# Borders of expert runs: half tiles, two side by side in the array, their weights copied ahead

## The chip, the core and the metric

The kernel runs on one core of a Trainium2 chip. Its engines are TensorE (PE in the profile, with its weight loads as PEld), VectorE (DVE), ScalarE (ACT), GpSimd (POOL) and SyncE (SP). The metric is the device time of one execution in microseconds; lower is better.

## The reference

A gated cross-attention block over `x` of shape (4, 512, 256) is followed by a feed-forward layer, which itself holds self-attention, an RMS norm, a shared gated network and a routed network. Only the routed network and the end matter here. Each of the 2048 tokens has two of eight experts, both of one group of four:

```python
p_expert = e_probs * g_prob
topv, topi = jax.lax.top_k(p_expert, TOPK)
w = jnp.zeros((S, E), flat.dtype).at[jnp.arange(S)[:, None], topi].set(topv)
h = _swiglu(flat @ W1_shared)
routed = jnp.zeros_like(shared)
for e in range(E):
    routed = routed + h @ W2_experts[e] * w[:, e:e + 1]
out = x + (shared + routed).reshape(Bb, Tt, C)
return _rmsnorm(out, norm2_w)
```

`h` has 512 columns and each `W2_experts[e]` is 512x256.

## The kernel before

The pair of experts of a token is its class: 2 groups with 6 pairs each, 12 classes. The kernel sorts the tokens by class (a count by matrix products, an indirect DMA that scatters the rows, a load of the sorted rows) and cuts the sorted rows into 16 tiles of 128 tokens (`NT`). Classes are ordered so that in each of two lanes (first and second expert) the expert stays the same over a run of classes. There are 14 runs and so 12 borders between runs of a lane (`BORDERS`, pairs of a class and a lane).

For each tile two *base* products are made, one for each lane, with the experts that hold at the tile's first row (`ebase`, read into registers by PE). A token of that tile that belongs to a later run gets weight 0 in the base product (`wb` against `wrest`). What is missing is added by the borders. A border lies in some tile that is known only at run time (`btile`); this tile's `h` is copied by ACT to a fixed place (`hb`, four places, 11 copies in all since two borders share a class), PE multiplies all of its 128 rows with the expert behind the border (an expert known in advance), and DVE adds the product to the sorted rows with the weights `wsel`, which are 0 for all rows but those of the run.

Sizes: `h` is stored as `hS`, 128 partitions x 16 tiles x 4 x 128 columns in fp32. A product is four matrix products over 4 x 128 rows of the contraction, each of 256 columns, and an fp32 matrix product shows as two instructions. So a base tile is 16 instructions and a pair of borders 16.

Each engine has its own list of instructions, written out by hand and coupled by semaphores. The order of PE's work at the end stands in the list `LAST`: the routed networks of four batches (`routed`), then base tile 0, the six pairs of borders, base tiles 1 to 15. `ETILES` numbers the products in that order over the eight banks of PSUM, and PE takes a bank when the product eight places earlier has been emptied, by the engine named in `ETILES` ("A" is ACT, "V" is DVE). DVE does, in order: base 0, the borders, the sum of squares of tile 0, then for each further tile `base(t)`, `finish(t - 1)`, `squares(t)`. `base` adds the two lanes (lines 1406 and 1413), `squares` sums the squares (1418) and multiplies by the norm's weights (1427), `finish` applies the row scale and the residual (1433). GpSimd computes the row scale (787) and stores the finished rows by an indirect DMA (793).

ACT at this stage makes the tanh of each routed product (line 967), and at the very end the border copies (999 loads the tile's number into a register, 1000 copies). Behind the last gate (`gate`, lines 1381 and 1384 on DVE) there is no other work on ACT. `runs` on DVE (1349 to 1358) computes the tables from the class counts; it is done before the first routed product.

Of the kernel before, what the change touches and what calls it, by code (L numbers as in the profile page):

```python
# [14 lines left out]
P = 128  # L15
# [20 lines left out]
def flamingo_block(nc, x, ctx_in, g_xattn, g_ffn, wq, bq, wk, bk, wv, bv,  # L36
# [138 lines left out]
    COPIES = list(dict.fromkeys(c_ for c_, _ in BORDERS))  # L175
# [54 lines left out]
    with es:  # L230
# [30 lines left out]
        tabs = sb("tabs", [P, 6, NCLS], F32)  # L261
# [53 lines left out]
        hb = [t_.rearrange("p (c j) -> p c j", c=HT) for t_ in th]  # L315
# [20 lines left out]
        btile = sb("btile", [P, NCLS], I32)  # L336
        leq = sb("leq", [P, NT, NCLS], F32)
# [3 lines left out]
        wrest = sb("wrest", [P, NT, 2], F32)  # L341
        wsel = sb("wsel", [P, 2, 8], F32)
        tok = sb("tok", [P, NT], U32)
        ssq = sb("ssq", [P, NT], F32)
        rs = sb("rs", [P, NT], F32)

# [69 lines left out]
        s_hb = sem("border_tile_copied")  # L416
# [42 lines left out]
        BORDER_USED = {c_: EAT["borders", j_ // 2] + 1 for j_, (c_, _) in enumerate(BORDERS)}  # L459

        WRAW = [src[2][:, 0:CT, :], src[3][:, 0:CT, :], sa[0][:, 0:CT, :]]

        N_CST = 14 + 3 * (len(STARTS[0]) + len(STARTS[1]))
# [6 lines left out]
        def _(sp):  # L471
# [154 lines left out]

            for a in range(8):
                sp.wait_ge(s_st[a], 16 * NT // 8)
# [3 lines left out]
        def _(pool):  # L632
# [68 lines left out]
            def constants():  # L701
# [14 lines left out]
                pool.iota(tstart[:], pattern=[[P, NT]], base=0, channel_multiplier=0,  # L716
# [88 lines left out]
        def _(act):  # L805
# [169 lines left out]

            for name, *at in LAST:
                if name in ("turn", "sorted"):
                    end_turn(name, *at)
                elif name in ("nets", "routed"):
                    for p in range(HT):  # L980
                        if at[1] <= 2 * p < at[2]:
                            tanh((B * (name == "routed") + at[0]) * HT + p, name, at[0], p)
                    if (name, at[0]) == ("nets", 1) and at[2] == NETT:
# [20 lines left out]
        def _(dve):  # L1004
# [341 lines left out]
            def runs():  # L1346
# [4 lines left out]
                link(V.tensor_scalar(bs[:], bs[:], float(NT * P - 1), None, ALU.min))  # L1351
# [3 lines left out]
                link(V.tensor_copy(btile[:], bs[:]))  # L1355
                mark(V.tensor_reduce(rbe[:], t, AX.X, ALU.add))
                link(V.tensor_scalar(btile[:], btile[:], 7, None, ALU.logical_shift_right))
                mark(V.tensor_copy(ebase[:], rbe[:, 2:4, :]))
                ready(s_run)

            def sorted_weights():
# [4 lines left out]
                link(V.tensor_tensor(wb[:], rn, rbe[:, 0:2, :].rearrange("p x t -> p t x"), ALU.is_equal))  # L1366
                link(V.tensor_tensor(wb[:], wb[:], wv, ALU.mult))
                link(V.tensor_tensor(wrest[:], wv, wb[:], ALU.subtract))
                for lane in range(2):
                    t = tmp[:, 0:8 * NT].rearrange("p (r t) -> p r t", r=8)  # L1370
                    link(V.tensor_tensor(t, rn[:, :, lane].unsqueeze(1).to_broadcast([P, 8, NT]),
# [16 lines left out]
            def border(j):  # L1388
                r = end_full("borders", j)
                for i in range(2):  # L1390
                    c, lane = BORDERS[2 * j + i]
                    at = dve.value_load(btile[0:1, c:c + 1], min_val=0, max_val=NT - 1)
                    y = srows[:, bass.ds(at, 1), 0:D].rearrange("p o c -> p (o c)")
                    x = RUN[lane][c] - 1
                    ins = V.scalar_tensor_tensor(out=y, in0=r[:, i * D:(i + 1) * D], scalar=wsel[:, lane, x:x + 1], in1=y,
                                                 op0=ALU.mult, op1=ALU.add)
                    if i:
                        ins.then_inc(s_ev, 1)
                        end_settle("borders", j)
                    else:  # L1400
                        link(ins)
# [90 lines left out]
        def _(pe):  # L1492
# [352 lines left out]
            def borders():  # L1845
                for j in range(len(BORDERS) // 2):
                    o = end_take("borders", j)
                    for i in range(2):
                        c, lane = BORDERS[2 * j + i]
                        at = COPIES.index(c)  # L1850
                        pe.wait_ge(s_hb, at + 1)
                        last = product(o[:, i * D:(i + 1) * D], [(hb[at % 4][:, k, :], w2[:, k, CLASSES[c][lane], :]) for k in range(HT)])
                    last.then_inc(s_ef, 1)
# [83 lines left out]
```

## Time and profile before

| | |
|---|---|
| median of 3 runs | 771.36 us (771.14 to 774.34) |
| the profiled execution | 771.94 us |
| its span, first to last instruction | 769.8 us |
| busy in the span | PE 738.4, DVE 514.1, ACT 408.4, POOL 217.7 us |
| borders on PE | 20.88 us |
| the 15 base tiles behind them on PE | 51.96 us |

Times in the rows are microseconds from the span's start unless marked ns; `x16` is a number of instructions. In a timeline row the last bracket is the idle time of that engine before the instruction and what ended it. PE's ends are modelled.

### The profile page before, as it was taken

To read this page: it belongs to the slowest core of one execution; us is meant where nothing else is said; L and a number is where in the kernel's file an instruction comes from. 1 tells how busy PE (TensorE), PEld (TensorE's weight loads), DVE (VectorE), ACT (ScalarE), POOL (GpSimd) and SP (SyncE) were. 2 spreads that over 40 slices of the span, in tenths; PEclk is the share of its full clock that TensorE was granted. 3 is DMA by queue.
4 is the path that set the end of the run, shared out by engine and by line. 5 is a ranking of instruction groups with operands and counts; after the bars stand their busy time and mean duration, and the time that the engine had idled before them with its cause. 6 is when DMAs were issued, how large, how long until landed. Compare 5 with 4: busy or idle time off the path is not lost.

```text
span 769.8 us, 10338 instructions
## 1 busy us (share of the span) xinstructions
PE 738.4 (96%) x3512; PEld 336.5 (44%) x3512; DVE 514.1 (67%) x774; ACT 408.4 (53%) x768; POOL 217.7 (28%) x327
## 2 busy tenths in 40 slices
PE   8889999999999999999999999999999999999995
PEld 5432343343233233233423432424544756468884
DVE  5698748847968878878797789771466122533765
ACT  4456867867758766875775867676211122222000
POOL 5252133223315405303321510010104631400444
PEclk9999999999999999999999999999999999999998
DMA  9519243325224414512331243005002565000011
GB/s 263 182 46 297 70 124 112 83 66 194 57 49 163 120 42 124 152 43 82 124 84 42 96 111 84 1 2 190 29 1 107 191 201 164 1 1 0 33 38 41
DMA packets 51891, 73.31 MB, mean 95 GB/s; under 512 B 7808, under 2 KB 42880, under 8 KB 51840
## 3 DMA queue, kind: packets, MB, share of 16 engines
q1 hardware_dynamic: 47248, 63.80, 28.4%
q0 software_dynamic: 2816, 8.46, 2.9%
q10 hardware_dynamic: 1776, 0.40, 0.3%
q8 instruction: 29, 0.48, 0.3%
q14 instruction: 22, 0.18, 0.1%
HBM read 45.04 MB, written 27.33 MB: 94 GB/s over the span
## 4 chain that ended last, share of the span: by engine, by line
PE 75%; DVE 13%; ACT 5%; issue 3%; DMA 3%; SPq 0%; POOL 0%; POOLq 0%; DVEq 0%; ACTq 0%
PE ps L1534 35%; PE ps L1693 12%; PE ps L1729 11%; PE ps L1665 10%; DVE negm L1180 8%; ACT hS L931 3%; PE ps L1529 2%; DVE bst L1058 1%; PE ps L1593 1%; PE ps L1679 1%; DMA rows<-in_L_xattn_wq_dram 1%; DMA w<-mTs 1%; PE ps L1588 1%; PE ps L1624 0%; DMA scrq<-mix 0%
## 5 line engine op out<-in xcount | busy, mean ns | idle before, releaser
L1180 DVE TENSOR_REDUCE negm<-ps 128x2 f32<-128x1024 f32 x256 | 303.6, 1220 | 72.7 <-PE ps L1665 64.9
L931 ACT ACTIVATE hS<-ps 128x512 f32<-128x512 f32 x512 | 280.7, 605 | 114.5 <-PE ps L1729 112.5
L1729 PE MATMUL ps<-w 98*128 98x512 bf16 x512 | 169.3, 383 | 6.4 <-DVE qk L1113 1.9
L1665 PE MATMUL ps<-w 96*128 96x512 bf16 x512 | 152.7, 379 | 8.0 <-DVE negm L1180 4.9
L1693 PE MATMUL ps<-hS,mix 128*17 128x512 f32 x1024 | 134.7, 598 | 0.2
L1729 PEld LDWEIGHTS ps<-w 98*128 98x128 bf16 x512 | 43.6, 96 | 157.3 <-ACT hS L931 94.8
L1665 PEld LDWEIGHTS ps<-w 96*128 96x128 bf16 x512 | 47.2, 98 | 60.1 <-DVE negm L1180 12.8
L1381 DVE SCALAR_TENSOR_TENSOR ctxs<-qk,ps 128x512 f32<-128x512 f32 x32 | 22.0, 687 | 71.5 <-ACT qk L967 46.0
L967 ACT ACTIVATE qk<-ps 128x512 f32<-128x512 f32 x32 | 19.1, 597 | 76.2 <-PE ps L1534 73.3
L1534 PE MATMUL ps<-w,hS 128*128 x256 | 55.6, 379 | 0.0
L1534 PEld LDWEIGHTS ps<-w,hS 128*128 128x128 f32 x256 | 48.6, 190 | 7.0 <-issue 0.5
L654 POOL TENSOR_TENSOR mdif<-bst 128x4 f32<-128x4 f32 x12 | 2.5, 205 | 150.6 <-DVEq L1020 150.6
L677 POOL TENSOR_TENSOR qk<-qk,mix 128x1024 f32<-128x1024 f32 x14 | 29.8, 2129 | 47.8 <-ACT mix L851 47.4
L692 POOL TENSOR_SCALAR hS<-hS,tg 128x256 f32<-128x256 f32 x16 | 14.9, 928 | 92.8 <-DVEq L1206 92.8
L1693 PEld LDWEIGHTS ps<-hS,mix 128*17 128x17 f32 x1024 | 17.0, 95 | 53.9 <-ACT hS L931 29.9
L672 POOL TENSOR_TENSOR qk<-qk,hT 128x1024 f32<-128x1024 f32 x8 | 18.8, 2348 | 76.1 <-DVEq L1020 76.1
L682 POOL TENSOR_TENSOR mix<-qk,mix 128x1024 bf16<-128x1024 f32 x14 | 29.9, 2134 | 21.9 <-ACT mix L855 20.8
L1534 PE MATMUL ps<-fout,hS 128*128 128x256 f32 x128 | 28.7, 380 | 1.5 <-issue 1.5
L1384 DVE SCALAR_TENSOR_TENSOR hS<-ctxs,ps 128x512 f32<-128x512 f32 x32 | 22.0, 687 | 11.8 <-PE ps L1534 10.6
L1534 PE MATMUL ps<-cT,fin 128*128 128x512 f32 x64 | 28.4, 594 | 0.3 <-ACT cT L960 0.3
L1534 PE MATMUL ps<-rope_sb,fin 128*128 128x512 f32 x64 | 28.4, 594 | 0.0
L1534 PE MATMUL ps<-wT,fin 128*128 128x512 f32 x64 | 28.1, 592 | 0.0
(217 smaller groups left out, 852.7 us busy)
## 6 DMA issues: line engine op xcount, KB each, us to landing
w<-scrq SPq DMA_DIRECT2D x32, 384.0 KB, 4.2
scrk<-mix SPq DMA_DIRECT2D x24, 256.0 KB, 2.3
scrq<-mix SPq DMA_DIRECT2D x16, 384.0 KB, 3.3
w<-scrk SPq DMA_DIRECT2D x32, 192.0 KB, 2.9
scrq<-mix SPq DMA_DIRECT2D x24, 256.0 KB, 2.6
w<-scrk SPq DMA_DIRECT2D x32, 128.0 KB, 3.0
w<-in_L_ffn_W_experts_dram SPq DMA_DIRECT2D x8, 512.0 KB, 8.2
mix<-scrf SPq DMA_DIRECT2D x4, 528.0 KB, 4.2
```

The costliest lines, as they stand in the source:

```text
L672: link(pool.tensor_tensor(qk[X][:], qk[X][:], rb[X], ALU.add))
L677: link(pool.tensor_tensor(qk[X][:], qk[X][:], parts[X][:, 0], ALU.subtract))
L682: link(pool.tensor_tensor(parts[X][:, 2], qk[X][:], parts[X][:, 1], ALU.subtract))
L931: nc.scalar.activation(prob[:, kt % PROB_SLOTS, s % HG, :], slot_bank(("unit", u)), ACT.Exp, scale=SC).then_inc(s_exp, 1)
L967: nc.scalar.activation(th[k % 4], end_full(f"{name}{b}", 2 * p), ACT.Tanh, scale=0.5).then_inc(s_th, 1)
L1180: V.tensor_reduce(negm[:, gi % 2, h, 2 * t2:2 * t2 + 2], ps[:, bank:bank + 2, :], AX.X, ALU.max, negate=True).then_inc(s_re, 1)
L1381: V.scalar_tensor_tensor(out=uu[:, k % 2, :], in0=th[k % 4], scalar=1.0, in1=end_full(f"{name}{b}", 2 * p), op0=ALU.add, op1=ALU.mult).the ...
L1384: V.scalar_tensor_tensor(out=hS[:, b * TT:(b + 1) * TT, p, :], in0=uu[:, k % 2, :].rearrange("p (t j) -> p t j", t=TT), scalar=0.5, in1=en ...
L1534: last = MM(o, w, r, start=(j == 0), stop=(j == len(terms) - 1))
L1665: last = MM(ps[:, bank + t, :], qs[0:STK, g, h, tt * P:(tt + 1) * P], ks[0:STK, g, h, :], start=True, stop=True)
L1693: last = MM(ps[32 * h:32 * h + VM, 6, :], vp[n % 2][:, kt, g * HG + h, :], prob[:, kk % PROB_SLOTS, h, :], start=(kt == 0), stop=(kt == TT ...
L1729: MM(o, ks[:, g, h, kt * P:(kt + 1) * P], qs[:, g, h, :], start=True, stop=True).then_inc(s_sT, 1)
```

## The change

Base tiles take the experts at their middle row (`tstart` begins at 64) instead of the first. A run that ends in a tile then misses rows either ahead of the border in the tile's first half, or behind it in the second half; only one half of 64 rows (`bhalf`) needs a correction. Which expert this half needs, the one ahead of the border or behind it, now depends on the half (`bexpi`). So each border takes a half tile of `h` (64 columns of the array) and two borders stand side by side in the array's columns 0 to 63 and 64 to 127, products of the two in turn.

Since the expert is known only at run time, ACT copies its weights (128 x 1024 elements) to a fixed place for each border (`wplace`), nine of them between the tanhs of the routed products, three after the half-tile copies at the end. The half-tile copies are 12 to 12 places, each with two register loads. ACT empties PSUM for the borders, two copies of 64 rows a pair, and SP doubles the 64 rows into the other 64 partitions by two DMAs a pair; DVE adds from there (`corr`). Base tile 1 moves ahead of the borders on PE and DVE.

```diff
-    LAST += [("base", 0), ("borders",)] + [("base", t_) for t_ in range(1, NT)]
+    LAST += [("base", 0), ("base", 1), ("borders",)] + [("base", t_) for t_ in range(2, NT)]
...
-            take_end("borders", range(len(BORDERS) // 2), "V")
+            take_end("borders", range(len(BORDERS) // 2), "A")
...
+            for q in range(len(BORDERS) // 2):
+                sp.wait_ge(s_ea, end_emptied("borders", q)[1])
+                sp.dma_start(corr[2 * q][HP:P, :], corr[2 * q][0:HP, :]).then_inc(s_br[q], 16)
+                sp.dma_start(corr[2 * q + 1][0:HP, :], corr[2 * q + 1][HP:P, :]).then_inc(s_br[q], 16)
...
-                pool.iota(tstart[:], pattern=[[P, NT]], base=0, channel_multiplier=0,
+                pool.iota(tstart[:], pattern=[[P, NT]], base=HP, channel_multiplier=0,
...
+                        pool.memset(tabs[:, 6 + lane, c:end], float(CLASSES[c][lane])).then_inc(s_cst, 1)
...
+            def border_weights(i):
+                if i == 0:
+                    act.wait_ge(s_run, 1)
+                    act.wait_ge(s_w2, 16 * NE)
+                if i < 2:
+                    act.wait_ge(s_ef, EAT[f"nets{B - 1}", NETT - 1] + 1)
+                elif i < 5:
+                    act.wait_ge(s_ef, EAT[f"routed{i - 2}", NETT - 1] + 1)
+                elif i < 9:
+                    act.wait_ge(s_y, B)
+                else:
+                    act.wait_ge(s_ef, EAT[f"routed{B - 1}", NETT - 1] + 1)
+                c, lane = BORDERS[i]
+                e = act.value_load(bexpi[0:1, lane, c:c + 1], min_val=0, max_val=NE - 1)
+                nc.scalar.activation(wplace[i], w2[:, :, bass.ds(e, 1), :].rearrange("p k o n -> p k (o n)"), ACT.Copy).then_inc(s_wc, 1)
+            WEIGHTS_AT = {(0, 1): [0], (0, 3): [1], (1, 1): [2], (2, 1): [3], (3, 0): [4], (3, 1): [5, 6], (3, 2): [7, 8]}
...
-            act.wait_ge(s_run, 1)
             act.wait_ge(s_ev, gate_done(2 * B * HT - 1))
-            for j, c in enumerate(COPIES):
-                if j >= 4:
-                    act.wait_ge(s_ef, BORDER_USED[COPIES[j - 4]])
+            for i, (c, lane) in enumerate(BORDERS):
                 at = act.value_load(btile[0:1, c:c + 1], min_val=0, max_val=NT - 1)
-                nc.scalar.activation(hb[j % 4], hS[:, bass.ds(at, 1)].rearrange("p o c j -> p (o c) j"), ACT.Copy).then_inc(s_hb, 1)
+                h = act.value_load(bhalf[0:1, c:c + 1], min_val=0, max_val=1)
+                nc.scalar.activation(hb[i], halves[:, bass.ds(at, 1), :, bass.ds(h, 1), :].rearrange("p t c h j -> p (t c) (h j)"),
+                                     ACT.Copy).then_inc(s_hb, 1)
+            for i in range(9, len(BORDERS)):
+                border_weights(i)
+            for q in range(len(BORDERS) // 2):
+                r = end_full("borders", q)
+                nc.scalar.activation(corr[2 * q][0:HP, :], r[0:HP, 0:D], ACT.Copy).then_inc(s_bc, 1)
+                nc.scalar.activation(corr[2 * q + 1][HP:P, :], r[HP:P, 0:D], ACT.Copy).then_inc(s_bc, 1)
+                act.wait_ge(s_bc, 2 * (q + 1))
+                act.sem_inc(s_ea, 1)
...
+            def border(i):
+                c, lane = BORDERS[i]
+                if i % 2 == 0:
+                    dve.wait_ge(s_br[i // 2], 32)
+                at = dve.value_load(btile[0:1, c:c + 1], min_val=0, max_val=NT - 1)
+                y = srows[:, bass.ds(at, 1), 0:D].rearrange("p o c -> p (o c)")
+                x = RUN[lane][c] - 1
+                link(V.scalar_tensor_tensor(out=y, in0=corr[i], scalar=wsel[:, lane, x:x + 1], in1=y, op0=ALU.mult, op1=ALU.add))
...
             base(0)
-            for j in range(len(BORDERS) // 2):
-                border(j)
+            base(1)
+            for i in range(len(BORDERS)):
+                border(i)
             squares(0)
-            for t in range(1, NT):
+            squares(1)
+            finish(0)
+            for t in range(2, NT):
...
+                for q in range(len(BORDERS) // 2):
+                    o = end_take("borders", q)
+                    pe.wait_ge(s_hb, 2 * q + 2)
+                    pe.wait_ge(s_wc, 2 * q + 2)
+                    for k in range(HT):
+                        for j in range(2):
+                            i = 2 * q + j
+                            last = MM(o[j * HP:(j + 1) * HP, 0:D], hb[i][:, k, :], wplace[i][:, k, :], start=(k == 0), stop=(k == HT - 1))
```

Left out of the diff: the places of `wplace`, `hb` and `corr` in tiles that are free by then, `runs` with some ten more operations of 12 or 24 elements for `bhalf` and `bexpi`, and `sorted_weights` with two more of 32 elements (rows ahead of the border now belong to the correction too).

## Rows read from the trace of the kernel before

**Rows 1.** The page's first part: busy time, share of the span, instructions.
```profile
PE 738.4 (96%) x3512; PEld 336.5 (44%) x3512; DVE 514.1 (67%) x774; ACT 408.4 (53%) x768; POOL 217.7 (28%) x327
```

**Rows 2.** The chain that ended last, from 560 us: start, us, what.
```profile
667.82 89.70 PE ps L1534 x376
```

**Rows 3.** Busy time by window: us, then each engine, clock, DMA share, GB/s.
```profile
691.74:712.40 20.66, 20.66 (x97) 18.21 (x96) 6.24 (x14) 4.41 (x7) 0.07 (x1) 1.00 0.00 0
```

**Rows 4.** Timeline, PE from base tile 0 on: start, us, instruction.
```profile
684.83 3.62 PE L1534 MATMUL ps<-w,hS 128*128 x16
...
688.28 20.88 PE L1534 MATMUL ps<-w,qk 128*128 128x256 f32 x96
...
709.00 51.96 PE L1534 MATMUL ps<-w,hS 128*128 x240
```

**Rows 5.** Timeline, DVE from the first squares to base tile 14.
```profile
711.77 0.43 DVE L1418 CUSTOM_DVE_ANT_0 tmp<-mix 128x256 f32<-128x256 f32 x1
...
712.54 0.42 DVE L1427 TENSOR_TENSOR hT<-mix,n_bc 128x256 f32<-128x256 f32 x1 [0.34 <-DVE ssq L1418]
712.88 0.48 DVE L1406 SCALAR_TENSOR_TENSOR mix<-ps,wb,mix 128x256 f32<-128x256 f32 x1
...
713.92 0.49 DVE L1433 SCALAR_TENSOR_TENSOR hT<-hT,rs,rows 128x256 f32<-128x256 f32 x1
...
715.17 0.46 DVE L1427 TENSOR_TENSOR hT<-mix,n_bc 128x256 f32<-128x256 f32 x1
...
757.55 0.48 DVE L1406 SCALAR_TENSOR_TENSOR mix<-ps,wb,mix 128x256 f32<-128x256 f32 x1 [0.70 <-PE ps L1534]
```

**Rows 6.** Timeline, PE in the router: the same round and the next.
```profile
555.52 0.59 PE L1789 MATMUL ps<-cT,fg 128*32 128x512 f32 x1
...
555.54 0.59 PE L1789 MATMUL ps<-nT,fg 128*32 128x512 f32 x1
555.95 0.59 PE L1789 MATMUL ps<-cT,fg 128*32 128x512 f32 x1
```

**Rows 7.** Timeline, the last gate and ACT's border copies.
```profile
685.10 0.69 DVE L1384 SCALAR_TENSOR_TENSOR hS<-ctxs,ps 128x512 f32<-128x512 f32 x1 [0.41 <-PE ps L1534]
686.75 2.57 ACT L1000 ACTIVATE qk<-hS 128x512 f32 x4 [2.79 <-DVE hS L1384]
...
700.40 0.63 ACT L1000 ACTIVATE qk<-hS 128x512 f32 x1 [0.31 <-issue]
```

**Rows 8.** Line 999, ACT's sequencer: ns min/median/max, first and last start.
```profile
L999 ACTq TENSOR_LOAD <-btile x11: 272/277/489, 685.9 to 703.0; - x11
L999 ACTq FUSED_REGOPS  x11: 152/152/185, 686.4 to 703.3; - x11
```

**Rows 9.** Line 855, ACT's copies of 128x1024.
```profile
L855 ACT ACTIVATE mix<-qk x14: 1047/1058/1088, 36.5 to 437.8; 128x1024 bf16<-128x1024 f32 x14
```

**Rows 10.** Timeline, ACT: one of the 16 routed tanhs.
```profile
679.93 0.60 ACT L967 ACTIVATE qk<-ps 128x512 f32<-128x512 f32 x1 [2.84 <-PE ps L1534]
```

**Rows 11.** Line 527, SP's DMAs of 256 KB: the issue, and the landing.
```profile
L527 SPq DMA_DIRECT2D scrk<-mix x24: 359/360/1435, 16.1 to 443.8; - x24
...
DMA to landing us min/median/max: 2.1/2.3/7.8
```

**Rows 12.** DMA issues: KB each, median us to landing.
```profile
w<-scrk SPq DMA_DIRECT2D x32, 64.0 KB, 3.3
```

**Rows 13.** Line 1392, DVE's sequencer in the borders.
```profile
L1392 DVEq TENSOR_LOAD <-btile x12: 298/302/554, 692.0 to 710.5; - x12
```

**Rows 14.** Timeline, DVE: the first pair of borders.
```profile
693.02 0.48 DVE L1395 SCALAR_TENSOR_TENSOR mix<-ps,wsel,mix 128x256 f32 x1 [3.42 <-issue]
694.27 0.48 DVE L1395 SCALAR_TENSOR_TENSOR mix<-ps,wsel,mix 128x256 f32 x1 [0.77 <-DVE mix L1395]
```

**Rows 15.** Timeline, DVE: the first routed gate after the runs.
```profile
623.54 0.69 DVE L1381 SCALAR_TENSOR_TENSOR ctxs<-qk,ps 128x512 f32<-128x512 f32 x1 [23.04 <-PE ps L1534]
```

**Rows 16.** Timeline, POOL: the first work after the constants.
```profile
67.56 0.94 POOL L692 TENSOR_SCALAR hS<-hS,tg 128x256 f32<-128x256 f32 x1 [9.98 <-DVEq L1206]
```

More of the change, by code:

```diff
@@ L173, in flamingo_block @@
     assert sorted(BORDERS) == sorted((c_, lane) for lane in range(2) for c_ in STARTS[lane][1:])
-    COPIES = list(dict.fromkeys(c_ for c_, _ in BORDERS))
+    HP = P // 2
     ETILES = []
@@ L260, in flamingo_block @@
         upto = sb("upto", [NT * NCLS // 2, 2, NT * NCLS + NCLS], F32)
-        tabs = sb("tabs", [P, 6, NCLS], F32)
+        tabs = sb("tabs", [P, 8, NCLS], F32)
         tstart = sb("tstart", [P, NT], F32)
@@ L314, in flamingo_block @@
         ostage = hT[:].rearrange("p k (u c) -> p (k u) c", u=2)
-        hb = [t_.rearrange("p (c j) -> p c j", c=HT) for t_ in th]
+        halves = hS[:].rearrange("p t c (h j) -> p t c h j", h=2)
+        hb = [t_[:, i * HT * HP:(i + 1) * HT * HP].rearrange("p (c j) -> p c j", c=HT)
+              for t_ in th + [uu[:, 0, :], uu[:, 1, :]] for i in range(2)]
+        fins = [fin[:, i].rearrange("p k n -> p (k n)")[:, j * HT * D:(j + 1) * HT * D].rearrange("p (k n) -> p k n", k=HT)
+                for i in range(2) for j in range(2)]
+        wplace = fins[0:2] + [t_.rearrange("p k n -> p (k n)").rearrange("p (k n) -> p k n", k=HT) for t_ in xT[0:3]]
+        wplace += [rows[:, 4 * i:4 * i + 4, 0:D] for i in range(4)] + fins[2:4]
+        wplace += [xT[3].rearrange("p k n -> p (k n)").rearrange("p (k n) -> p k n", k=HT)]
         lg = sb("lg", [P, NT, NR], F32)
@@ L336, in flamingo_block @@
         btile = sb("btile", [P, NCLS], I32)
+        bhalf = sb("bhalf", [P, NCLS], I32)
+        bpos = sb("bpos", [P, 3, NCLS], F32)
+        bexp = sb("bexp", [P, 2, NCLS], F32)
+        bexpi = sb("bexpi", [P, 2, NCLS], I32)
         leq = sb("leq", [P, NT, NCLS], F32)
@@ L341, in flamingo_block @@
         wrest = sb("wrest", [P, NT, 2], F32)
+        bno = sb("bno", [P, NT, 2], F32)
         wsel = sb("wsel", [P, 2, 8], F32)
@@ L345, in flamingo_block @@
         rs = sb("rs", [P, NT], F32)
+        corr = [ostage[:, i, :] for i in range(8)] + [tmp[:, i * D:(i + 1) * D] for i in range(3)] + [oT[:, 0:D]]
         ps = es.enter_context(nc.psum_tensor("ps", [P, 8, L], F32))
@@ L415, in flamingo_block @@
         s_ssh = sem("sorted_shared_loaded")
-        s_hb = sem("border_tile_copied")
+        s_hb = sem("border_half_copied")
+        s_wc = sem("border_weights_copied")
+        s_bc = sem("border_product_copied")
+        s_br = [sem(f"border_rows_doubled{q}") for q in range(len(BORDERS) // 2)]
         s_ss = sem("squares_summed")
@@ L456, in gate_half @@
             return end_emptied(f"{name}{b}", 2 * p)[1]
-        BORDER_USED = {c_: EAT["borders", j_ // 2] + 1 for j_, (c_, _) in enumerate(BORDERS)}
         WRAW = [src[2][:, 0:CT, :], src[3][:, 0:CT, :], sa[0][:, 0:CT, :]]
-        N_CST = 14 + 3 * (len(STARTS[0]) + len(STARTS[1]))
+        N_CST = 14 + 4 * (len(STARTS[0]) + len(STARTS[1]))
         def group_inst(gi):
@@ L982, in _ @@
                             tanh((B * (name == "routed") + at[0]) * HT + p, name, at[0], p)
+                            for i in WEIGHTS_AT.get((at[0], p), []) if name == "routed" else []:
+                                border_weights(i)
                     if (name, at[0]) == ("nets", 1) and at[2] == NETT:
@@ L1350, in runs @@
                                      bs[:].unsqueeze(1).to_broadcast([P, NT, NCLS]), ALU.is_ge))
-                link(V.tensor_scalar(bs[:], bs[:], float(NT * P - 1), None, ALU.min))
+                link(V.tensor_scalar(bs[:], bs[:], -1.0, 0.0, ALU.add, ALU.max))
                 t = tmp[:].rearrange("p (x t c) -> p x t c", x=4, t=NT)
@@ L1354, in runs @@
                                      tabs[:, 0:4, :].unsqueeze(2).to_broadcast([P, 4, NT, NCLS]), ALU.mult))
-                link(V.tensor_copy(btile[:], bs[:]))
+                mark(V.tensor_copy(btile[:], bs[:]))
+                link(V.tensor_copy(bhalf[:], bs[:]))
                 mark(V.tensor_reduce(rbe[:], t, AX.X, ALU.add))
-                link(V.tensor_scalar(btile[:], btile[:], 7, None, ALU.logical_shift_right))
+                mark(V.tensor_scalar(btile[:], btile[:], 7, None, ALU.logical_shift_right))
+                link(V.tensor_scalar(bhalf[:], bhalf[:], 6, None, ALU.logical_shift_right))
                 mark(V.tensor_copy(ebase[:], rbe[:, 2:4, :]))
+                mark(V.tensor_copy(bpos[:, 0], btile[:]))
+                link(V.tensor_copy(bpos[:, 1], bhalf[:]))
+                link(V.scalar_tensor_tensor(out=bpos[:, 2], in0=bpos[:, 0], scalar=-2.0, in1=bpos[:, 1], op0=ALU.mult, op1=ALU.add))
+                link(V.tensor_scalar(bpos[:, 2], bpos[:, 2], 1.0, None, ALU.subtract))
+                link(V.tensor_tensor(bexp[:], tabs[:, 2:4, :], bpos[:, 2:3, :].to_broadcast([P, 2, NCLS]), ALU.mult))
+                link(V.tensor_tensor(bexp[:], bexp[:], tabs[:, 6:8, :], ALU.add))
+                mark(V.tensor_copy(bexpi[:], bexp[:]))
+                link(V.tensor_scalar(bpos[:, 2], bpos[:, 2], 1.0, None, ALU.add))
+                mark(V.tensor_copy(bhalf[:], bpos[:, 2]))
                 ready(s_run)
@@ L1365, in sorted_weights @@
                 mark(V.tensor_copy(tok[:], srows[:, :, D + 4]))
-                link(V.tensor_tensor(wb[:], rn, rbe[:, 0:2, :].rearrange("p x t -> p t x"), ALU.is_equal))
+                rb_ = rbe[:, 0:2, :].rearrange("p x t -> p t x")
+                mark(V.tensor_tensor(bno[:], rn, rb_, ALU.is_lt))
+                link(V.tensor_tensor(wb[:], rn, rb_, ALU.is_equal))
+                mark(V.tensor_tensor(bno[:], bno[:], rn, ALU.add))
                 link(V.tensor_tensor(wb[:], wb[:], wv, ALU.mult))
@@ L1386, in gate @@
                                        op0=ALU.mult, op1=ALU.mult).then_inc(s_ev, 1)
[L1388 to L1401, printed above, removed]
+            def border(i):
[6 more added lines that the diff above has]
+                link(V.scalar_tensor_tensor(out=y, in0=corr[i], scalar=wsel[:, lane, x:x + 1], in1=y, op0=ALU.mult, op1=ALU.add))
             def base(t):
@@ L1845, in borders @@
             def borders():
[L1846 to L1852, printed above, removed]
+                for q in range(len(BORDERS) // 2):
[6 more added lines that the diff above has]
+                            last = MM(o[j * HP:(j + 1) * HP, 0:D], hb[i][:, k, :], wplace[i][:, k, :], start=(k == 0), stop=(k == HT - 1))
                     last.then_inc(s_ef, 1)
```

3 lines of the change are left out of this document (2 added, 1 removed).

## The prediction

> **What bounds the kernel now.** I read the page's engine line first, then the chain of waits over the last 210 us, then the timeline of each engine from 684 us on. TensorE (PE) is busy in nearly the whole span [rows 1], and the chain of the last stage is one piece of PE products from 667.82 to 757.52 us [rows 2]. In that piece lie the last products of the routed nets, base tile 0, the six pairs of borders and base tiles 1 to 14 and half of 15. The stretch of the borders is full of PE, while VectorE (DVE) works 6 us and ScalarE (ACT) 4 us of its 21 [rows 3]. PE spends 20.88 us on the 96 border products, 3.45 us a pair, and 51.96 us on the 15 later base tiles, 3.46 us each [rows 4].
>
> So a saving on PE counts only as far as DVE can follow, and DVE's own pace decides that. DVE sits idle 0.70 us before each late base tile, until PE's product is there; tile 14 begins at 757.55. A base tile that DVE had not to wait for is tile 1: it begins at 712.88, 0.34 us after the start of the operation before it (L1427), and its own L1427 begins at 715.17 [rows 5]. So DVE alone needs 715.17 - 712.88 + 0.34 = 2.63, say 2.65 us a tile: it can win back 0.8 us a tile on PE, and no more.
>
> **PE's part.** Each pair becomes two products of 64 columns in the two halves of the array. No row shows 64 columns. The nearest is the router, four products of 32 columns each: their instructions begin at 555.52 to 555.54, and the next round at 555.95 [rows 6], so four run in the time of one, 0.43 us for 512 elements. For two halves of 256 elements I take one in the time of two: 20.88 becomes 10.4 us. The bounds are 10.4 and 20.9 (no gain). Base tile 1 now comes ahead of the borders, which start two tiles after 684.83, at 691.74 [rows 4], and without waits would end at 702.1.
>
> **ACT's part, which I think sets the end.** Before, ACT made 11 copies of whole tiles, four of them before PE needed the first. Now it makes, after the last gate: 12 copies of half tiles, each with two indices loaded from memory into registers; three copies of weights (borders 9, 10, 11); and only then the 12 copies of products out of PSUM. These all stand in order on one engine. Step by step:
>
> The last gate ends at 685.10 + 0.69 = 685.79 and ACT's first copy starts at 686.75; four copies take 2.57 us [rows 7]. As the copy itself is 0.63, the step from one to the next is (2.57 - 0.63) / 3 = 0.65. 
> Of weights, ACT has 128x1024 copies at 1.06 us [rows 9]. One load (0.65), then three copies: 700.6 + 0.65 + 3.18 = 704.4. The nine other weight copies go between the tanhs, where ACT idles 2.84 us after each 0.60 us [rows 10]; one or two copies (1.1 or 2.1 us, their index loads under the tanh before) fit. Without that cover each would cost 1.06.
>
> The product copies are 64x256 out of PSUM: from 0.60 for 512 elements [rows 10], less 256 elements at (1.06 - 0.63) / 512 us, 0.39 each. Two of them and ACT's signal are ready at 705.2.
>
> **The DMA's part.** SyncE doubles each pair's rows with two transfers of 64 KB. Its shortest transfers land 2.1 us after issue, median 2.3, and an issue takes 0.36 [rows 11]; transfers of this size took 3.3 in a queue of others [rows 12]. Nothing else is on the queue here, so I take 2.2 + 0.4 = 2.6: rows doubled at 707.8. Bounds 2.5 and 3.7. Queued behind that wait on SP are only later pairs and the last waits for the stores. Later pairs are ready every 0.8 us, faster than DVE takes them.
>
> **DVE's part.** DVE has been idle since base tile 1 (some 14 us). Its first border needs an index load, about 1.0 us after the wait; borders then follow at 694.27 - 693.02 = 1.25 us, because each load waits for the chain behind the border before [rows 13, 14]. The reads now come from SBUF instead of PSUM; DVE's L1433, which reads two SBUF tiles, also takes 0.49 [rows 5], so the price stays. Twelve borders: 707.8 + 1.0 + 11 x 1.25 + 0.48 = 723.0. Then squares of tiles 0 and 1 (1.11 us each, as 711.77 to 712.88 [rows 5]) and finish 0 (0.49, with its waits 0.65) bring base tile 2 to 725.9. Twelve tiles at 2.65 make 31.8: base tile 14 at 757.7, against 757.55 now. Everything behind it is as it was.
>
> To this I add two holes of 0.31 us, as the one that ACT shows under "issue" among eleven copies [rows 7], since ACT's list of instructions here grows two to three times: 0.6. Sum: +0.15 + 0.6, some 0.8 us. PE meanwhile waits for weights 9 to 11, ends the borders at 704.4 + 1.7 = 706.1 and base tile 14 at 751.2, so about 6 us of its gain lie idle before DVE's tile 14. PSUM does not hold PE: base tile 10 needs tile 2's bank, which DVE empties near 727, and PE is there at 733.7.
>
> **Costed at nothing.** The longer computation of the runs on DVE, some ten operations of 0.2 us, falls before an idle time of 23.04 us [rows 15]. The 14 new memsets on GpSimd, 0.1 us each, fall before an idle time of 9.98 us [rows 16]. Two more operations on the sorted rows' weights (0.4) fall into DVE's waits for PE.
>
> **A rule against the change.** ACT's index loads take 277 ns and DVE's 302 ns [rows 8, 13]. The Trainium skill, page "DMA: Bandwidth & Descriptors", section "Latency and other measured facts", gives a floor of about 600 ns for a tensor_load; by that the path's 25 loads on ACT and 12 on DVE would add 25 x 0.32 + 12 x 0.30 = 11.7 us, an estimate of 784.5 us. Both rows are about half of that floor, so the trace does not bear it out; the third rival below is its mechanism, priced from rows.
>
> **Rivals.**
>
> *PE stays the bound.* Then the full 10.4 us count: 761.5. DVE would have to reach base tile 2 by 757.5 - 10.4 - 31.8 = 715.3 us, 10.6 us before my sum. The order on ACT alone speaks against it: its first product copy comes no sooner than the three late weights. Chance 0.03.
>
> *The second index load is hidden.* At 0.65 a copy, ACT is ready 12 x 0.56 = 6.7 us sooner and DVE stays the bound: 772.7 - 6.7 = 766.0. For it: ACT's load begins while the copy before it runs. Against it: the step of 0.65 is already as long as its register work. Chance 0.05.
>
> *Slower: the index loads at their first price.* The first load of each engine took 489 (ACT) and 554 ns (DVE) [rows 8, 13]. If loads of three alternating tables always cost that, 25 x 0.21 + 12 x 0.25 = 8.3 us more: 781. It passes the 0.5% once the 37 loads are longer by 0.08 us each. Against it: the medians, 277 and 302, over eleven and twelve loads at changing addresses. Chance 0.10.
>
> *The halves don't run side by side.* Then PE ends the borders at 712.4 and base tile 14 at 757.5, level with DVE's chain: no change or 1 us more, about 772. The time does not show it; the timeline of PE would. Chance 0.05.
>
> *My sum:* 0.77.
>
> **The numbers.** The sum goes onto the profiled execution: 771.94 us, of which 769.8 are span. With 0.8 more it is 772.7. The runs' median, 771.36, lies 0.6 below that execution, so the forecast is 772.2. Within 0.5% (about what a measurement of this kernel can tell from no change) means 767.5 to 775.2. Faster than that: the first two rivals, 0.07 (the second lies just beyond the bound, so not all of its 0.05 counts). Slower: 0.13, the third rival's 0.10 and 0.03 for the sum with several upper ends together (transfers at 3.7, +1.1; a third and fourth hole, +0.6; loads 0.05 longer, +1.8). Same: 0.80. The range that leaves out no more than 2 in 10 is 768.0 to 776.3: below, half of the second load hidden (-3.4) and a little; above, those upper ends.
>
> **What would show it.** PE: border instructions in twos, a pair in 1.7 us, a wait of some 3.5 us before the fifth pair and 0.4 to 2 before the sixth. ACT: copies of half tiles 1.2 us apart from 687.3 to 700.6, then three copies of weights, the first product copy at 704.4. DVE: idle until about 708.8, borders 1.25 apart to 723, then base tiles 2.65 apart with no wait for PE. I am wrong if DVE still waits for PE in the base tiles, if the half-tile copies come closer than 1.0 or farther than 1.4 us apart, or if the first border on DVE begins before 705 or after 712.

## The result, and the profile after

| | before | after |
|---|---|---|
| median, 20 runs each | 772.62 us | 775.04 us (772.47 to 778.54) |
| ratio to before | | 1.0034, 95% interval 1.0023 to 1.0046 |
| span of the profiled execution | 769.8 us | 772.8 us |

The changed kernel is 2.6 us slower by the ratio (0.0034 x 772.6). The forecast was 0.8 us slower, "same" within 0.5%, range 768.0 to 776.3.

I split the 3.0 us between the two spans at points that both traces have. Behind the end of the last gate the change behaves nearly as predicted. More than half of the difference between these two executions lies ahead of that gate, where no step of the prediction looks. Outside its span the changed kernel needs 0.4 us less (774.58 - 772.8 = 1.78 us, where the kernel before has 771.94 - 769.8 = 2.14), so the two profiled times lie 2.6 us apart; the profile does not show why.

| point | before | after | after, a second execution |
|---|---|---|---|
| last gate ends | 685.79 | 687.43 | 685.71 |
| from there to base tile 14 on DVE | 71.76 | 72.89 | 72.62 |
| from there to the end of the span | 12.25 | 12.48 | 12.57 |
| span | 769.8 | 772.8 | 770.9 |

The first part of the page of the changed kernel answers to [rows 1]: PE is 6.2 us less busy, DVE has 13 instructions more, ACT 25 and POOL 14.

```profile
PE 732.2 (95%) x3512; PEld 327.3 (42%) x3512; DVE 514.3 (67%) x787; ACT 423.1 (55%) x793; POOL 218.6 (28%) x341
```

**PE.** This is the timeline of PE in the changed kernel: base tiles 0 and 1, then the first pairs of borders and the fifth.

```profile
686.47 7.07 PE L1599 MATMUL ps<-w,hS 128*128 x32
693.47 1.95 PE L1918 MATMUL ps<-fin,qk 128*64 128x256 f32 x16
695.25 0.38 PE L1918 MATMUL ps<-cT,qk 128*64 128x256 f32 x1
695.25 0.38 PE L1918 MATMUL ps<-rope_sb,qk 128*64 128x256 f32 x1
695.46 0.38 PE L1918 MATMUL ps<-cT,qk 128*64 128x256 f32 x1
...
696.97 0.38 PE L1918 MATMUL ps<-wT,qk 128*64 128x256 f32 x1
...
704.54 0.40 PE L1918 MATMUL ps<-rows,ctxs 128*64 128x256 f32 x1 [3.95 <-ACT fin L1013]
...
705.67 0.63 PE L1918 MATMUL ps<-rows,ctxs 128*64 128x256 f32 x1
```

The second pair begins at 695.25 and the third at 696.97: 1.72 us a pair where [rows 4] have 3.45. The two products of a pair start together (695.25 and 695.25), and the next instruction of the first product follows 0.21 later, as in a product that has the array to itself. Then PE waits 3.95 us for the first of the three late copies of weights on ACT (L1013). Behind that wait an instruction shows 0.63 instead of 0.38 us from 705.67 on. The windows (columns as in [rows 3]) say why: the granted clock is 1.00 ahead of the wait, and behind it 0.68 on average over a stretch that ends with full-speed instructions again, so in part of it PE ran at the lower of its two levels (1.2 instead of 2.4 GHz). Here that costs nothing, since DVE is late anyway. The sixth pair follows the fifth without a wait.

```profile
693.50:700.50 7.00, 7.00 (x65) 4.47 (x64) 0.97 (x2) 2.45 (x6) 0.00 (x0) 1.00 0.00 0
704.50:709.80 5.30, 5.25 (x32) 3.65 (x32) 0.00 (x0) 4.72 (x11) 0.00 (x0) 0.68 0.15 36
```

**ACT.** The timeline of ACT in the changed kernel, half-tile copies (L1042), late weights (L1013) and the first product copy (L1048); it answers to [rows 7].

```profile
688.71 0.42 ACT L1042 ACTIVATE qk<-hS 128x256 f32 x1 [3.10 <-issue]
689.97 0.42 ACT L1042 ACTIVATE qk<-hS 128x256 f32 x1 [0.85 <-issue]
...
702.68 0.42 ACT L1042 ACTIVATE ctxs<-hS 128x256 f32 x1 [0.86 <-issue]
703.34 2.00 ACT L1013 ACTIVATE fin<-w 128x1024 f32 x2 [0.25 <-issue]
705.25 1.04 ACT L1013 ACTIVATE nT<-w 128x1024 f32 x1
706.20 0.36 ACT L1048 ACTIVATE hT<-ps 64x256 f32<-64x256 f32 x1
```

A copy of 0.42 us stands every 1.27 us ((702.68 - 688.71) / 11); between copies ACT waits 0.85 us for its own sequencer. What the sequencer does then is in the groups of its lines (nanoseconds: shortest, median, longest), first the load of the tile's number and its evaluation, then the address of the copy:

```profile
L1040 ACTq TENSOR_LOAD <-btile x12: 275/277/283, 687.5 to 701.4; - x12
L1040 ACTq FUSED_REGOPS  x12: 147/158/158, 687.8 to 701.7; - x12
...
L1042 ACTq FUSED_REGOPS  x12: 136/136/142, 688.5 to 702.5; - x12
```

The load of the half (L1041) takes 277 ns and its evaluation 147. Together these five make 1.0 of the 1.27 us.

**SP and DVE.** SP's first doubling in its timeline, the issue; the seven issues behind it that begin before 712 us take 0.59 to 0.61, the ninth 1.12.

```profile
707.03 0.50 SPq L644 DMA_DIRECT2D hT<-hT  x1
```

The timeline of DVE shows the first borders, the last, the two squares, and base tiles 2 and 14; it answers to [rows 5, 14].

```profile
710.67 0.48 DVE L1463 SCALAR_TENSOR_TENSOR mix<-hT,wsel,mix 128x256 f32 x1 [16.03 <-issue]
711.93 0.48 DVE L1463 SCALAR_TENSOR_TENSOR mix<-hT,wsel,mix 128x256 f32 x1 [0.77 <-DVE mix L1463]
...
714.61 0.48 DVE L1463 SCALAR_TENSOR_TENSOR mix<-hT,wsel,mix 128x256 f32 x1 [0.94 <-DVE mix L1463]
...
724.61 0.48 DVE L1463 SCALAR_TENSOR_TENSOR mix<-oT,wsel,mix 128x256 f32 x1 [0.76 <-DVE mix L1463]
...
726.27 0.43 DVE L1489 TENSOR_TENSOR hT<-mix,n_bc 128x256 f32<-128x256 f32 x1 [0.71 <-DVE ssq L1480]
...
728.38 0.48 DVE L1468 SCALAR_TENSOR_TENSOR mix<-ps,wb,mix 128x256 f32<-128x256 f32 x1
...
760.32 0.47 DVE L1468 SCALAR_TENSOR_TENSOR mix<-ps,wb,mix 128x256 f32<-128x256 f32 x1
```

From 710.67 on DVE never waits for PE until base tile 14: the bracket that [rows 5] show there (0.70, PE) is gone. Base tiles come every 2.66 us ((760.32 - 728.38) / 12).

**Ahead of the gate.** The views below are the timeline of PE in the output products of the shared net (`fout`), first in the kernel before, then in the changed one.

```profile
609.75 0.38 PE L1534 MATMUL ps<-fout,hS 128*128 128x256 f32 x1 [0.79 <-issue]
610.48 0.38 PE L1534 MATMUL ps<-fout,hS 128*128 128x256 f32 x1 [0.35 <-issue]
611.18 1.56 PE L1534 MATMUL ps<-fout,hS 128*128 128x256 f32 x6 [0.33 <-issue]
612.58 1.04 PE L1529 MATMUL ps<-identf,mix 128*128 128x128 f32 x8
613.45 5.78 PE L1534 MATMUL ps<-fout,hS 128*128 128x256 f32 x26
```

```profile
607.73 0.48 PE L1599 MATMUL ps<-fout,hS 128*128 128x256 f32 x1 [0.34 <-issue]
609.14 0.38 PE L1599 MATMUL ps<-fout,hS 128*128 128x256 f32 x1 [0.93 <-issue]
609.85 4.53 PE L1599 MATMUL ps<-fout,hS 128*128 128x256 f32 x11 [0.33 <-issue]
614.22 1.04 PE L1594 MATMUL ps<-identf,mix 128*128 128x128 f32 x8
615.09 4.27 PE L1599 MATMUL ps<-fout,hS 128*128 128x256 f32 x19
```

Both kernels stall here for three short times of which the profile names no cause ("issue"), 1.47 us together before and 1.60 after. But in the changed kernel the 11 instructions behind the stalls take 4.53 us, some 0.4 each: half pace. Over 607 to 616 us the granted clock is 1.00 before and 0.81 after (0.50 to 0.52 from 610 to 613 us, the lower of the two levels):

```profile
607.00:616.00 9.00, 7.54 (x38) 6.09 (x37) 0.00 (x0) 2.66 (x5) 4.47 (x6) 1.00 0.68 193
```

```profile
607.00:616.00 9.00, 7.33 (x28) 5.23 (x27) 0.00 (x0) 2.66 (x5) 4.56 (x6) 0.81 0.63 192
```

The products behind the eight transposes (L1529, L1594) begin at 613.45 before and at 615.09 after. From there to the end of the last gate both need 72.34 us. So the whole 1.64 us between the gates is there when these transposes end, the changed lines of the last stage have no part in it, and the nine copies of weights between the tanhs cost nothing. The stretch itself lost more: PE begins the `fout` products at 596.71 before and at 596.15 after, so from there to the products behind the transposes it needs 16.74 us before and 18.94 after, 2.20 more.

### The profile page after: what moved, and what is told of

Same layout as the page of the kernel before. It is cut to its first block, busy times and chain, and to the rows that moved or that the text cites. A ratio compares the mean times of both kernels' runs of the same rounds, so it can differ in the third digit from the quotient of the medians.

```text
span 772.8 us, 10497 instructions
## 1 busy us (share of the span) xinstructions
PE 732.2 (95%) x3512; PEld 327.3 (42%) x3512; DVE 514.3 (67%) x787; ACT 423.1 (55%) x793; POOL 218.6 (28%) x341
## 4 chain that ended last, share of the span: by engine, by line
PE 66%; DVE 18%; ACT 6%; issue 4%; DMA 2%; ACTq 1%; DVEq 1%; POOL 1%; SPq 0%; POOLq 0%
PE ps L1599 26%; PE ps L1758 12%; PE ps L1794 11%; PE ps L1730 10%; DVE negm L1231 8%; ACT hS L952 3%; PE ps L1594 2%; DVE bst L1109 2%; PE ps L1658 1%; PE ps L1744 1%; DVE hT L1495 1%; DVEq L1460 1%; DVE mix L1475 1%; DVE tmp L1480 1%; DVE mix L1463 1%
## 5 line engine op out<-in xcount | busy, mean ns | idle before, releaser
L702 POOL TENSOR_TENSOR mix<-qk,mix 128x1024 bf16<-128x1024 f32 x14 | 29.8, 2132 | 21.9 <-ACT mix L876 20.9
L1599 PE MATMUL ps<-fout,hS 128*128 128x256 f32 x128 | 30.7, 396 | 1.7 <-issue 1.6
L1452 DVE SCALAR_TENSOR_TENSOR hS<-ctxs,ps 128x512 f32<-128x512 f32 x32 | 22.0, 688 | 10.3 <-PE ps L1599 9.2
L1599 PEld LDWEIGHTS ps<-fout,hS 128*128 128x128 f32 x128 | 25.2, 198 | 7.4 <-issue 4.0
```

The lines of the kernel that those rows point to most:

```text
L702: link(pool.tensor_tensor(parts[X][:, 2], qk[X][:], parts[X][:, 1], ALU.subtract))
L1452: V.scalar_tensor_tensor(out=hS[:, b * TT:(b + 1) * TT, p, :], in0=uu[:, k % 2, :].rearrange("p (t j) -> p t j", t=TT), scalar=0.5, in1=en ...
L1599: last = MM(o, w, r, start=(j == 0), stop=(j == len(terms) - 1))
```

## The experiments

The theory behind my sum: the halves do run side by side and PE's gain is real, but the time to the end is set by loads of indices into registers, two a copy on ACT and one a border on DVE, and by the order of ACT's list. Rivals: PE is still the bound; the second load costs nothing; the halves don't run side by side. All these kernels compute the whole output.

**Products of a pair not in turn.** In the changed kernel the instructions of the two halves alternate. Here each product stands whole.

```diff
-                    for k in range(HT):
-                        for j in range(2):
+                    for j in range(2):
+                        for k in range(HT):
```

> The changed kernel, with the two halves of a pair on PE one after the other (all four products of the first border, then all four of the second) instead of in turn. Theory (ACT's copies and then DVE set the end, PE has about 9 us to spare at base tile 14): PE needs 3.45 us a pair again, ends the borders near 714 instead of 709.7, and the time stays within 1 us of the changed kernel's, so 2 to 4 us above the kernel before. Rival (PE is still the bound and its saving is real but lost elsewhere): up to 10 us more, 13 above the kernel before.

775.81 us, ratio to before 1.005 (1.0032 to 1.0067). It did not separate the halves, which it was meant to do. PE's timeline shows the second product of one pair beside the first product of the next:

```profile
697.00 0.43 PE L1918 MATMUL ps<-cT,qk 128*64 128x256 f32 x1
697.21 0.38 PE L1918 MATMUL ps<-fin,qk 128*64 128x256 f32 x1
697.27 0.38 PE L1918 MATMUL ps<-cT,qk 128*64 128x256 f32 x1
697.42 0.38 PE L1918 MATMUL ps<-fin,qk 128*64 128x256 f32 x1
```

So here two products in different halves overlapped when both stood next in PE's list; the order by turns is not needed. Base tile 14 begins 72.92 us behind the gate, as in the changed kernel; of the 1.8 us between the two spans 1.7 lie ahead of the gate again. To take the gain away, both borders must use the same half; that is the sixth experiment.

**DVE loads its twelve indices early**, behind base tile 1, where it is idle for 16 us.

```diff
-                at = dve.value_load(btile[0:1, c:c + 1], min_val=0, max_val=NT - 1)
...
+            ats = [dve.value_load(btile[0:1, c_:c_ + 1], min_val=0, max_val=NT - 1) for c_, _ in BORDERS]
             for i in range(len(BORDERS)):
-                border(i)
+                border(i, ats[i])
```

> The changed kernel, with DVE loading the tile numbers of all twelve borders into registers while it is idle ahead of the first border, instead of one behind each border. Theory: the borders on DVE no longer cost 1.25 us each but 0.52, until SyncE's two transfers a pair (1.28 us a pair) set the pace; DVE is done with the borders 7 us sooner, then catches up with PE near the last base tiles. 5 us below the changed kernel, 2 to 3 below the kernel before. Rival (the end is set by PE or by what lies ahead of the borders): within 1 us of the changed kernel.

770.25 us, ratio 0.9978 (0.9961 to 0.9994): 4.8 below the changed kernel, as expected. Borders come 0.63 apart until they wait for SP's transfers:

```profile
710.60 1.11 DVE L1462 SCALAR_TENSOR_TENSOR mix<-hT,wsel,mix 128x256 f32 x2 [0.23 <-DMA hT<-hT]
713.30 2.37 DVE L1462 SCALAR_TENSOR_TENSOR mix<-hT,wsel,mix 128x256 f32 x4 [1.58 <-DMA hT<-hT]
```

Half of the 1.25 us of a border on DVE was the load that stood in the chain. From base tile 12 on DVE waits 0.70 us a tile for PE again, so PE sets the end of this version.

**ACT copies the first four pairs' products ahead of the late weights.**

```diff
-            for i in range(9, len(BORDERS)):
-                border_weights(i)
             for q in range(len(BORDERS) // 2):
+                if q == 4:
+                    for i in range(9, len(BORDERS)):
+                        border_weights(i)
```

> The changed kernel, with ACT copying the products of the first four pairs out of PSUM ahead of the three late copies of weights instead of behind them. Theory (the order on ACT delays DVE): the first border on DVE 3.2 us sooner, PE's last two pairs 2 us later, 3 us below the changed kernel, level with the kernel before. Rival (the delay comes from the transfers or from DVE's own pace alone): under 1 us.

775.05 us, ratio 1.0039 (1.002 to 1.0057): no gain, a miss. DVE's first border did come 3.2 us sooner (20.04 behind the gate). But the weights came later, PE waited 7.81 us for the first of them, and its next instructions took 0.63 instead of 0.38 us; the granted clock was 0.59 over 706 to 716 us (windows):

```profile
708.17 0.66 PE L1919 MATMUL ps<-rows,ctxs 128*64 128x256 f32 x1 [7.81 <-ACT fin L1013]
```

```profile
706.00:716.00 10.00, 7.83 (x38) 5.12 (x39) 3.44 (x8) 4.68 (x8) 0.00 (x0) 0.59 0.23 53
```

PE ended the borders 27.5 us behind the gate, where I had expected 24.5, and base tile 14 waits for PE at 72.70. The gain moved from DVE's chain into PE's. I had reckoned PE's pairs at full speed.

**One index for a half tile**: tile and half are put into one number on DVE, in `runs`, so ACT has one load and a simpler address.

```diff
-                h = act.value_load(bhalf[0:1, c:c + 1], min_val=0, max_val=1)
-                nc.scalar.activation(hb[i], halves[:, bass.ds(at, 1), :, bass.ds(h, 1), :].rearrange("p t c h j -> p (t c) (h j)"),
-                                     ACT.Copy).then_inc(s_hb, 1)
+                at = act.value_load(bhalf[0:1, c:c + 1], min_val=0, max_val=8 * NT - 7)
+                nc.scalar.activation(hb[i], blocks[:, bass.ds(at, 7), :][:, 0:7:2, :], ACT.Copy).then_inc(s_hb, 1)
```

> The changed kernel, with one index a half-tile copy (8 x tile + half, worked out on DVE) instead of two. Theory (register work of 1.27 us sets the pace of ACT's twelve copies): the copies come 0.71 us apart, all is 6.5 us sooner from there on, 6 us below the changed kernel, 3 to 4 below the kernel before. Rival (the copies themselves, or PE, set the pace): the step stays over 1 us or the time stays within 1 us of the changed kernel.

767.74 us, ratio 0.9943 (0.9922 to 0.9964): 7.3 below the changed kernel. ACT's timeline, and the address's group on its sequencer:

```profile
688.67 0.42 ACT L1042 ACTIVATE qk<-hS 128x256 f32 x1 [0.23 <-issue]
689.31 0.42 ACT L1042 ACTIVATE qk<-hS 128x256 f32 x1 [0.22 <-issue]
```

```profile
L1042 ACTq FUSED_REGOPS  x12: 46/46/46, 687.9 to 695.0; - x12
```

The step falls from 1.27 to 0.64. The second load goes with its evaluation (277 + 147 ns), and the address falls from 136 to 46 ns; the rest, some 0.1 us, lies between the instructions. The second load was not hidden.

**Both of these together.** The edits of the second and the fourth experiment.

> The changed kernel with one index a half-tile copy on ACT and with DVE's tile numbers loaded ahead of the first border, both together. Theory (index loads on ACT and DVE hold back a saving that PE has made): the first border on DVE 8 us sooner, the twelve of them in 7 us instead of 14, so that PE is the bound again from about base tile 6 on: base tile 14 on DVE 62 us after the last gate instead of 72.9, 10 us below the changed kernel, 8 to 9 below the kernel before. Rival (the saving on PE is not real, or something behind the borders is the bound): no lower than the one-index kernel alone.

764.33 us, ratio 0.9908 (0.9892 to 0.9924). This version beats both kernels: 7.1 us below the one before by the ratio, where I had expected 8 to 9, and its median is 10.7 below that of the changed one. From the gate to the end of the span it needs 74.29 us, the kernel before 84.01: 9.7 less; but its gate ends 1.4 us later, as the granted clock fell in the stretch of 607 to 616 us here too. DVE reaches base tile 2 at 27.16 us behind the gate, and from tile 11 on (I had expected 6) it waits for PE again:

```profile
738.60 0.48 DVE L1467 SCALAR_TENSOR_TENSOR mix<-ps,wb,mix 128x256 f32<-128x256 f32 x1 [0.18 <-PE ps L1599]
742.06 0.48 DVE L1467 SCALAR_TENSOR_TENSOR mix<-ps,wb,mix 128x256 f32<-128x256 f32 x1 [0.70 <-PE ps L1599]
```

**The same with both borders in one half of the array.** ACT's and SP's copies follow to the other place.

```diff
-                    for k in range(HT):
-                        for j in range(2):
+                    for j in range(2):
+                        for k in range(HT):
-                            last = MM(o[j * HP:(j + 1) * HP, 0:D], hb[i][:, k, :], wplace[i][:, k, :], start=(k == 0), stop=(k == HT - 1))
+                            last = MM(o[0:HP, j * D:(j + 1) * D], hb[i][:, k, :], wplace[i][:, k, :], start=(k == 0), stop=(k == HT - 1))
```

> The kernel of both edits, but with the two borders of a pair in the same half of the array (columns 0 to 63), side by side in the bank instead of in the array, so that they can't run at once. Theory: the borders take 20.7 us on PE again, and as PE is the bound in the kernel of both edits, all 10 us come back: 9 to 11 us above it, level with the kernel before. Rival (PE's saving plays no part in the gain): under 2 us above it.

775.34 us, ratio 1.0034 (1.0022 to 1.0045): 11.0 above the fifth. In the two profiles 10.3 us lie behind the gate (84.63 us from there to the end, beside 74.29), level with the 84.01 of the kernel before. PE's timeline has products one behind the other, 1.73 us each, and ACT's product copies wait for them:

```profile
700.91 1.89 PE L1918 MATMUL ps<-cT,qk 128*64 128x256 f32 x8
702.64 1.89 PE L1918 MATMUL ps<-rope_sb,qk 128*64 128x256 f32 x8
```

```profile
708.02 0.38 ACT L1047 ACTIVATE hT<-ps 64x256 f32<-64x256 f32 x1 [2.81 <-PE ps L1918]
```

PE's borders take 20.9 us here and 10.6 in the fifth experiment. So once DVE and ACT keep up, the saving on PE is worth its full size.

**The changed kernel with both borders in one half**, and nothing else.

> The changed kernel with nothing but the two borders of a pair in the same half of the array, one after the other. The kernel with the halves in turn did not do this: its products still ran in both halves at once. Theory: PE ends the borders 27 us after the last gate instead of 22.5, base tile 14's product at 72, just ahead of DVE, so the time stays within 1.5 us of the changed kernel. Rival (PE is the bound): 4 us or more above it.

774.55 us, ratio 1.0033 (1.002 to 1.0046): the same as the changed kernel, though PE does 20.86 us of borders instead of 10.4 and its wait. Base tile 14 begins 72.79 us behind the gate, and DVE waits for PE at none of the base tiles behind the borders. PE's saving is not on the path in the changed kernel, so PE is not its bound.

**The kernel before and the changed kernel, each once more with a profile**, for the stretch at 607 to 616 us.

> The kernel before, once more, for the place where PE stands still about 608 us after the start, ahead of everything that the change moves. If its length varies by itself, the last gate ends 1 to 2 us later than the 685.8 us of the first profile; if the change makes it longer, it ends within 0.7 us of that.

> The changed kernel once more, one look. The stage behind the last gate should repeat within 0.1 us: half-tile copies 1.27 apart, first border on VectorE 23.2 us behind the gate's end, base tile 14 at 72.9. The open point is the stretch 607 to 616 us. If the change lengthens it always, the granted clock falls below 1.00 there again and the last gate ends at 686.8 or later (687.4 in the first profile); if the first profile was only an unlucky execution, the clock stays 1.00 and the gate ends near 685.8 or sooner, as in both profiles of the kernel before (685.8 and 684.8).

The kernel before: 770.97 us, clock 1.00 there, products behind the transposes at 612.47, gate end 684.81. That is 1.0 us sooner than in its first profile, which neither branch of the expectation has: the stretch varies by itself. The changed kernel: 772.6 us beside 771.8 of the kernel before, clock 1.00 as well:

```profile
607.00:616.00 9.00, 7.57 (x37) 5.81 (x36) 0.00 (x0) 2.66 (x5) 4.73 (x6) 1.00 0.68 194
```

Its products behind the transposes begin at 613.37 and its gate ends at 685.71, as in the first profile of the kernel before. Then the changed kernel is 0.8 us slower, the forecast's number (one execution of each): 1.2 by the spans, less the 0.4 outside them. So the change does not lengthen that stretch always. Over all profiles: in six of the nine executions of changed programs the granted clock fell in it (the first of the changed kernel and the first, fourth, fifth, sixth and seventh experiment), in neither of the two of the kernel before. The other three of the nine begin these products at 613.37, 614.68 and 614.85. From the first `fout` product on the stretch takes 18.87 to 19.33 us in the six and 16.35 to 17.41 in the five whose clock stayed at 1.00, so the fall costs some 2 us. The length of the stalls alone does not decide it: together they last 1.60 to 2.35 us in the six, 1.02 to 2.14 in the five.

The timed runs say how usual this is, as each has its mean granted clock on record. Of the 20 of the changed kernel two have 0.991, as its second profile, where the clock fell only behind PE's wait for the late weights, and take 772.47 and 772.78 us; the other 18 have 0.984 to 0.990 and take 773.88 to 778.54. The kernel before loses clock at times too: 43 of its runs, taken beside the experiments, have the clock on record, and 21 of them have 0.996 to 0.998, as its two profiles, and take 770.71 to 772.34 us, the other 22 have 0.992 to 0.995 and take 772.16 to 777.03. So both profiles of the kernel before are of executions that kept the clock, and against those the second profile of the changed kernel, and the two runs like it, are about 1 us slower. The mean does not tell where in a run the clock fell.

## Why the prediction was right or wrong

**PE's part: right.** 1.72 us a pair, taken as half of 3.45; the wait for the fifth pair is 3.95, "some 3.5". The wait of 0.4 to 2 us before the sixth pair did not show: the fifth ran in part at the lower clock and took 2.5 us, and by then the sixth's weights were there. The sixth and seventh experiments show both sides of the saving: 10.3 us behind the gate where PE is the bound, nothing where it is not.

**ACT sets the end: right, the copy step a little small.** 1.27 us for 1.21, within 0.65 to 1.42. The load and its evaluation cost what I took (0.43). The rest, taken as 0.13, is 0.19; the address with two indices (136 ns for 46, the fourth experiment) is about half of that rest. The first product copy stands 18.77 us behind the gate; 18.6 was predicted.

**The DMA's part: right in sum.** An issue of half a tile takes 0.50 to 0.61 (one 1.12), not 0.36, and the landing 2.2 as taken. DVE's first border begins 23.2 us behind the gate, 23.0 predicted.

**DVE's part: right, some 0.7 us short of its own.** Borders 1.25 apart with one hole of 0.17. The squares behind them are longer than taken, 3.3 us from the last border's end to base tile 2 instead of 2.9: L1489 waits 0.71 for the sum and not 0.34. Twelve tiles at 2.66 for 2.65 add 0.1. Base tile 2 comes at 40.95 for 40.1, of which 0.2 came from the engines ahead of DVE.

**The two holes of 0.31 on ACT: not there**, in neither execution. They happened to cover most of what the other terms were short, by luck. The stage's sum was +0.8; it measured +1.4 in the first profile (1.13 to base tile 14 and 0.23 behind it) and +1.2 in the second.

**What the sum left out: everything ahead of the last gate.** The prediction took it as it was. That gate ended 1.64 us later in the profiled execution. The traces put this into the stretch with PE's stalls at 607 to 611 us: in six of nine changed executions the granted clock falls behind them, and PE's own list is not changed there. The items that the prediction costed at nothing do not show: PE reaches the stretch no later than before (596.15 and 596.41 us in the two executions, beside 596.71 and 596.12), and behind it the last gate ends 72.34 us later in both kernels. The prediction read no view of that stretch. Why the changed kernel loses clock there more often, as the timed runs suggest, is open. The stalls lie beside SP's load of the sorted rows and busy DMA engines (0.63 to 0.68 of the window in the four profiles of the two kernels), and the lists of ACT, DVE and POOL are longer; none of this was tried by itself.

So that 775.04 us lies within the range is in part luck: its upper end was made of longer transfers, more holes on ACT and longer loads, and what used that room was the clock. The 0.4 us outside the span, which the prediction took as fixed, went the other way.

**The rivals.** PE as the bound: refuted by the seventh experiment. A hidden second load: refuted by the step of 1.27 and by the fourth. Loads at their first price: refuted, 275 to 283 ns for twelve loads at changing addresses on ACT; on DVE the median is 308 ns and the longest 558. The floor of about 600 ns for a tensor_load, which the Trainium skill gives ("DMA: Bandwidth & Descriptors", section "Latency and other measured facts"), is again not borne out by these 277 ns. (The prediction's estimate by it is 772.7 + 11.7 = 784.4 us, not 784.5.) Halves that don't run side by side: refuted by PE's timeline.

## What to carry to other kernels

When an engine gets faster, price the engines that must follow in their own list's order, sequencer included: here an index load with its evaluation (0.43 us) twelve times on ACT and a load within a dependent chain (0.6 us) twelve times on DVE hid a saving of some 10 us on PE. Fold indices into one number where they are computed, and load them into registers while the engine is idle, before the wait. And look for stretches far from the change where an engine that sets the end stands still without a named cause; a different program may lose more there.

## What the runs showed that I had not expected

PE's granted clock fell to its lower level behind waits, and instructions took 0.63 instead of 0.38 us: behind 3.95 us of waiting from about 705.5 to 709.0, behind 7.81 us from 708.17 to 713.8, and behind the short stalls at 607 to 614 us, with a few instructions between them, in six of eleven profiles. Behind the 2.68 us that PE waits for the late weights in the first experiment it did not fall. In four profiles (first, third, sixth and seventh experiment) it also fell near 31 us, behind a wait of 2.0 to 3.0 us for a DMA: 0.83 over 30 to 40 us, in the sixth 0.66. In the other seven that wait is 1.97 to 3.32 us, and it did not fall. So the length of one wait does not tell it. A wait on PE can thus cost more than its length, as in the third experiment.

Products of 64 columns in different halves run together without being issued in turn (the first experiment).
